# Softmax sums of a cross-attention block inverted on VectorE in four columns instead of as a power on POOL, and P's high part taken one step later on ScalarE

## The chip, the cores and the metric

One core of a Trainium2 chip runs the whole program. The metric is the device time of one execution in microseconds (us). The engines of the core work side by side, each through its own list of instructions in order: TensorE (PE in the profile; PEld is its weight load), VectorE (DVE), ScalarE (ACT), GpSimd (POOL), and SyncE (SP), whose queue issues every DMA of this kernel. They wait for each other only by semaphores.

## The reference

```python
x = x + xattn(layernorm(x), ctx, ctx, w_q, w_k, w_v, w_out, mask)
x = x + ffn(layernorm(x), w12, b12, w3, b3)

def xattn(q, k, v, ...):      # 16 batches, 128 rows, D = 1024, 32 heads of 32, 8 groups of 4 heads
    query, key, value = q @ w_q.T, k @ w_k.T, v @ w_v.T
    scores = einsum('bghnd,bgsd->bghns', query, key) / 32 ** 0.5
    attention = softmax(where(mask, scores, min), axis=-1)
    out = einsum('bghns,bgsd->bghnd', attention, value)
    return out @ w_out.T

def ffn(x, w12, b12, w3, b3): # M = 1024
    x1, x2 = split(x @ w12.T + b12, 2)
    return (silu(x1) * x2) @ w3.T + b3
```

All tensors are float32 with x of (16, 128, 1024). The kernel keeps float32 accuracy by splitting each operand of a product into a high and a low float16 part, and takes three products (high by high, high by low, low by high).

## The kernel before

**Blocks and steps.** The attention part runs over eight blocks of two batches (256 rows). A block has eight steps, one for each group of four heads; g counts the steps of all blocks, 0 to 63. The loop on every engine is the same, for t in 1 to 8 and s in 0 to 7 with g = 8 (t - 1) + s. In round t the attention of block t - 1 is done together with the projections (q, k, v) of block t and the output projection of block t - 2. Behind round 8 comes the feed-forward part.

**One step on TensorE** (L1623 to L1650): the eight score products of g (L1468), a first unit, the product of P and v of step g - 3 (weigh, L1474), and a second unit. A unit is a projection of 24 products. Steps 3 to 6 have one of the output projection, which is twice as long. Step 7 has the two v units and four groups of transposes of new x rows (turn_x, L1415) between them. The results go to five PSUM banks in turn; begin (L1381) waits until the bank's last reader is done. The scores have one PSUM tile only, so the scores of g wait for VectorE to have read those of g - 1 (s_neg, L1465).

**A step's softmax** goes over four engines. The tile e has two buffers, g % 2.
- VectorE masks and scales the scores into e, four heads of a batch u and then four of the other (mask_scores, L1884, instructions L1895). It waits first until the low part of P of g - 2 has been taken from the same buffer (s_plo2, L1893).
- ScalarE takes the exponents (exps, L1201; L1207 where it also sums them into p_sum) for u = 0, then does other work of the step, then u = 1.
- For g in 8 to 47 (NORMED, L72) P is divided by its sum here, scaled by 2**14. In steps 0 and 1 VectorE does it (norm_prob, L1908), in steps 2 to 7 POOL (norm_prob, L975). POOL takes three instructions for each u: p_sum times 2**-14 (L979), that to the power -1 (L981), and the product with e (L985).
- ScalarE takes P's high part (prob_hi, L1213, L1222) at the end of its step g.
- POOL takes the low part (prob_lo, L969, L972) at the head of its step g + 1.
- SP then issues the DMA that transposes both (turn_prob, L727), and TensorE uses them in step g + 3.

**What else stands in the queues.** POOL splits the next block's ctx in steps 0 and 1 (split_ctx, L928, its instructions L904, L906, L908) and takes the rows' roots in steps 2 and 3. SP's list of a step (L786 to L834) puts turn_prob(g - 1) ahead of the step's loads: the q and k stacks, ctx of the next block in step 3, and in rounds 3 to 6 the loads of a piece of the feed-forward weights (load_look) in steps 0, 3 and 5. VectorE takes the maximum of these pieces (max_of, L1729, its instruction L1731) in steps 2, 4 and 6, in its place in the list, ahead of the second unit's low part and of the next mask_scores. ScalarE normalises the next rows with scale_rows (L1295), after prob_hi in steps 4 and 6; the rows are turned by TensorE in step 7.

Of the kernel before, what the change touches and what calls it, by code (L numbers as in the profile page):

```python
# [22 lines left out]
F32 = mybir.dt.float32  # L23
# [8 lines left out]
P = 128  # L32
# [7 lines left out]
U = 2  # L40
# [281 lines left out]

def divided_count(g):

    return g + 1 - normed_count(g)
# [16 lines left out]
def xattn_ffn(nc, x, ctx_t, mask, wq_t, wk_t, wv_t, wo_t, w12_t, b12_t, w3_t, b3_row, out):  # L342
# [8 lines left out]
    with ExitStack() as stack:  # L351
# [82 lines left out]
        inv_pool = part(arena_attn, 60, 1, F32)[:, 0:U * HPG].rearrange("p (u j) -> p u j", u=U)  # L434
        minus_one = part(arena_attn, 62, 1, F32)[:, 0:1]
        inv_vector = part(arena_attn, 61, 1, F32)[:, 0:U * HPG].rearrange("p (u j) -> p u j", u=U)
# [154 lines left out]
        s_minus_one = sem("minus_one_done")  # L591
        s_pinv, s_pnorm = sem("pool_inv_sum_done"), sem("prob_normed_by_pool")
        s_vinv, s_vnorm = sem("vector_inv_sum_done"), sem("prob_normed_by_vector")
# [301 lines left out]
        def _(pool):  # L895
# [57 lines left out]
            pool.memset(minus_one, -1.0).then_inc(s_minus_one, 1)  # L953
            pool.wait_ge(s_minus_one, 1)
# [20 lines left out]
            def norm_prob(g):  # L975
                n = normed_count(g - 1, by_pool)
                for u in range(U):
                    pool.wait_ge(s_exp, 2 * g + u + 1)
                    pool.tensor_scalar(inv_pool[:, u], p_sum[:, g % 2, u], 1 / P_SCALE, None, ALU.mult).then_inc(s_pinv, 1)  # L979
                    pool.wait_ge(s_pinv, 2 * (U * n + u) + 1)  # L980
                    pool.tensor_tensor(inv_pool[:, u], inv_pool[:, u], minus_one.broadcast_to([P, HPG]), ALU.pow)\  # L981
                        .then_inc(s_pinv, 1)
                    pool.wait_ge(s_pinv, 2 * (U * n + u) + 2)
                    heads = e[:, g % 2, u].rearrange("p (j n) -> p j n", j=HPG)
                    ins = pool.tensor_tensor(heads, heads, inv_pool[:, u].rearrange("p (j o) -> p j o", o=1)  # L985
                                             .broadcast_to([P, HPG, SEQ]), ALU.mult)
                ins.then_inc(s_pnorm, 1)

            halves = range(2), range(2, 4)
            for t in range(1, NB + 1):  # L990
                for s in range(STEPS):
                    if GROUPS * (t - 1) + s > PLO_ALONE:
                        prob_lo(GROUPS * (t - 1) + s - 1)
                    if by_pool(GROUPS * (t - 1) + s):
                        norm_prob(GROUPS * (t - 1) + s)
# [84 lines left out]
        def _(act):  # L1080
# [132 lines left out]
            def prob_hi(g):  # L1213
                if by_pool(g):
                    act.wait_ge(s_pnorm, normed_count(g, by_pool))
# [93 lines left out]
            for t in range(1, NB + 1):  # L1309
                for s in range(STEPS):  # L1310
                    g, (tile, tile2) = GROUPS * (t - 1) + s, x_tiles(t, s)
                    exps(g, 0)
                    if t == NB and s - 1 in H_AT:
                        hid_hi(0, H_AT[s - 1])
# [17 lines left out]
                    prob_hi(g)  # L1332
# [345 lines left out]
        def _(dve):  # L1678
# [228 lines left out]

            def norm_prob(g):  # L1908
                n = normed_count(g - 1, by_vector)
                for u in range(U):  # L1910
                    dve.wait_ge(s_exp, 2 * g + u + 1)
                    dve.reciprocal(inv_vector[:, u], p_sum[:, g % 2, u]).then_inc(s_vinv, 1)
                    dve.wait_ge(s_vinv, U * n + u + 1)
                    heads = e[:, g % 2, u].rearrange("p (j n) -> p j n", j=HPG)
                    ins = dve.scalar_tensor_tensor(out=heads, in0=heads, scalar=P_SCALE,
                                                   in1=inv_vector[:, u].rearrange("p (j o) -> p j o", o=1)
                                                   .broadcast_to([P, HPG, SEQ]), op0=ALU.mult, op1=ALU.mult)
# [156 lines left out]
            for t in range(1, NB + 1):  # L2074
# [7 lines left out]
                for s in range(STEPS):  # L2082
                    g, name, (tile, tile2) = GROUPS * a + s, top_at(t, s), x_tiles(t, s)
# [163 lines left out]
```

## Time and profile before

| what | us |
|---|---|
| median of 3 runs | 1074.25 (1072.92 to 1075.79) |
| the profiled execution | 1076.37 |
| its span | 1074.6 |
| PE busy | 1026.1 (95%) |
| VectorE busy | 670.4 (62%) |
| ScalarE busy | 473.2 (44%) |
| POOL busy | 644.7 (60%) |

The span runs from the first to the last instruction; the rest of the profiled time lies around it. Busy is the time in which an engine has an instruction in work. Matmuls are pipelined, so a busy PE is not PE at its peak. The shares are averages over parts with different limits: the feed-forward part fills the second half of the span, and the rounds that the change touches lie between about 113 us and 472 us.

### The profile page before, as it was taken

Reading aid. Unit: us, or ns where it says so; the run is one execution under the profiler, and the core shown is the slowest. Engines: PE = TensorE matmul, PEld = TensorE weight load, DVE = VectorE, ACT = ScalarE, POOL = GpSimd, SP = SyncE. Lnnn points to the kernel's source line nnn. Section 1 sums busy time; section 2 is a strip of 40 time slices with the busy share of each in tenths; the row PEclk is TensorE's granted clock in tenths of the full one; section 3 lists DMA queues with packets and bytes.
Section 4 is the critical chain, followed back from the end, with each engine's and each line's share of the span. In section 5 each row is a group of like instructions: output and inputs, shape, how many; then the busy total and the mean of one; then the engine's idle time right before and its main releaser. Section 6 shows DMA issues by size and latency. Waiting matters only on the chain.

```text
span 1074.6 us, 22142 instructions
## 1 busy us (share of the span) xinstructions
PE 1026.1 (95%) x8320; PEld 683.5 (64%) x8320; DVE 670.4 (62%) x2040; ACT 473.2 (44%) x1303; POOL 644.7 (60%) x657
## 2 busy tenths in 40 slices
PE   8898899998979989989999999999999999999998
PEld 7786757766658557677755544444444788468853
DVE  6889976767677667777856523735766255635431
ACT  5767566656566556666566511123432011301110
POOL 2769877987978879878985879226862201203000
PEclk8998999998999989989999999999999999999999
DMA  9569676897798788969994552397649731774201
GB/s 370 212 171 190 152 193 166 175 249 198 193 219 217 206 210 176 254 173 237 231 255 79 136 218 94 134 271 255 225 164 226 267 113 55 196 238 135 80 30 49
DMA packets 230779, 199.13 MB, mean 185 GB/s; under 512 B 177040, under 2 KB 187280, under 8 KB 225808
## 3 DMA queue, kind: packets, MB, share of 16 engines
q1 hardware_dynamic: 230672, 197.72, 67.1%
q8 instruction: 66, 1.08, 0.4%
q14 instruction: 41, 0.34, 0.1%
HBM read 119.04 MB, written 35.65 MB: 144 GB/s over the span
## 4 chain that ended last, share of the span: by engine, by line
PE 61%; POOL 19%; ACT 5%; DVE 4%; issue 4%; DMA 1%; SPq 1%; DVEq 0%; POOLq 0%; ACTq 0%
PE bank_dense L1411 38%; PE bank_spare L1411 7%; PE bank_score L1567 6%; PE bank_spare L1567 5%; POOL arena_attn L972 5%; POOL arena_attn L981 4%; POOL arena_attn L985 4%; PE bank_av L1567 3%; POOL arena_in L908 2%; ACT arena_attn L1207 2%; POOL arena_in L904 2%; ACT arena_attn L1222 2%; DVE arena_attn L1895 1%; POOL arena_in L906 1%; PE bank_score L1468 1%
## 5 line engine op out<-in xcount | busy, mean ns | idle before, releaser
L1411 PE MATMUL bank_dense<-arena_rows,arena_in 128*128 128x256 f16 (+1 forms) x1272 | 176.1, 296 | 1.6 <-POOL arena_in L908 0.9
L1411 PE MATMUL bank_dense<-arena_attn,arena_rows 128*128 128x512 f16 x768 | 166.4, 379 | 0.0
L1411 PEld LDWEIGHTS bank_dense<-arena_rows,arena_in 128*128 128x128 f16 x1272 | 122.1, 98 | 44.5 <-DVE arena_in L1743 1.3
L1895 DVE CUSTOM_DVE_ANT_0 arena_attn<-bank_score,arena_in 128x128 f32<-128x128 f32 x512 | 143.5, 344 | 0.7 <-PE bank_score L1468 0.5
L1411 PEld LDWEIGHTS bank_dense<-arena_attn,arena_rows 128*128 128x128 f16 x768 | 75.2, 98 | 90.1
L972 POOL TENSOR_TENSOR arena_attn<-arena_attn 128x512 f16<-128x512 f32 x89 | 103.3, 1177 | 46.8 <-ACT arena_attn L1222 46.8
L1207 ACT ACTIVATE arena_attn<-arena_attn,arena_in 128x128 f32<-128x128 f32 x320 | 123.7, 390 | 16.5 <-DVE arena_in L1895 16.5
L1411 PE MATMUL bank_dense<-arena_out,arena_attn 128*128 128x512 f16 x576 | 127.8, 379 | 0.5 <-DVE arena_attn L1937 0.5
L1222 ACT ACTIVATE arena_attn<-arena_attn 128x1024 f16<-128x1024 f32 x64 | 67.5, 1055 | 108.5 <-POOL arena_attn L985 96.8
L1411 PEld LDWEIGHTS bank_dense<-arena_out,arena_attn 128*128 128x128 f16 x576 | 55.5, 98 | 64.0 <-DVE arena_attn L1937 0.6
L1411 PE MATMUL bank_spare<-arena_rows,arena_in 128*128 128x256 f16 (+1 forms) x648 | 87.7, 292 | 0.0
L1411 PE MATMUL bank_dense<-arena_out,arena_in 128*128 128x512 f16 x384 | 83.0, 379 | 0.0
L908 POOL TENSOR_TENSOR arena_in<-arena_in 128x512 f16<-128x512 f32 x62 | 77.1, 1243 | 5.0
L1210 ACT ACTIVATE arena_attn<-arena_attn,arena_in 128x128 f32<-128x128 f32 x192 | 60.8, 391 | 34.1 <-DVE arena_in L1895 33.8
L1411 PEld LDWEIGHTS bank_spare<-arena_rows,arena_in 128*128 128x128 f16 x648 | 62.3, 98 | 19.8
L2000 DVE SCALAR_TENSOR_TENSOR arena_out<-bank_dense,small,arena_out 128x256 f32<-128x256 f32 x64 | 27.9, 478 | 74.9 <-PE bank_dense L1411 74.9
L1411 PEld LDWEIGHTS bank_dense<-arena_out,arena_in 128*128 128x128 f16 x384 | 37.6, 98 | 45.3
L1411 PE MATMUL bank_dense<-arena_in 128*128 128x256 f16 x456 | 64.4, 308 | 1.5 <-DVE arena_in L1750 1.4
L985 POOL TENSOR_TENSOR arena_attn<-arena_attn 128x512 f32<-128x512 f32 x60 | 62.4, 1039 | 4.7
L981 POOL TENSOR_TENSOR arena_attn<-arena_attn 128x4 f32<-128x4 f32 x60 | 62.1, 1035 | 5.0
L918 POOL TENSOR_TENSOR small<-small 128x1 f32<-128x1 f32 x32 | 20.2, 633 | 72.9 <-DVE small L1784 72.9
L1207 ACT ACTIVATION_READ_ACCUMULATOR arena_attn<-arena_attn,arena_in 128x1 f32 x320 | 60.6, 189 | 0.0
(237 smaller groups left out, 1942.1 us busy)
## 6 DMA issues: line engine op xcount, KB each, us to landing
arena_rows<-x SPq DMA_DIRECT2D x32, 512.0 KB, 5.4
arena_in<-w_scratch SPq DMA_DIRECT2D x64, 256.0 KB, 3.0
arena_attn<-q_scratch SPq DMA_DIRECT2D x48, 256.0 KB, 4.3
arena_rows<-w_t SPq DMA_DIRECT2D x12, 1024.0 KB, 6.4
arena_rows<-ctx_t SPq DMA_DIRECT2D x8, 1024.0 KB, 5.9
q_scratch<-arena_attn SPq DMA_DIRECT2D x16, 512.0 KB, 4.6
x_scratch<-arena_rows SPq DMA_DIRECT2D x16, 512.0 KB, 4.1
arena_out<-x_scratch SPq DMA_DIRECT2D x16, 512.0 KB, 5.7
```

What stands on the lines that cost most here:

```text
L904: pool.tensor_tensor(buf, src, spread, ALU.mult).then_inc(s_pool, 1)
L908: pool.tensor_tensor(lo, buf, hi, ALU.subtract).then_inc(ready, 1)
L972: ins = pool.tensor_tensor(p_split[:, g % 2, u, 1], e[:, g % 2, u], p_split[:, g % 2, u, 0], ALU.subtract)
L981: pool.tensor_tensor(inv_pool[:, u], inv_pool[:, u], minus_one.broadcast_to([P, HPG]), ALU.pow)\
L985: ins = pool.tensor_tensor(heads, heads, inv_pool[:, u].rearrange("p (j o) -> p j o", o=1) .broadcast_to([P, HPG, SEQ]), ALU.mult)
L1207: ins = act.activation(head, head, ACT.Exp, bias=neg_max[:, g % 2, h:h + 1], scale=-1.0, accum_out=p_sum[:, g % 2, u, j:j + 1])
L1210: ins = act.activation(head, head, ACT.Exp, bias=neg_max[:, g % 2, h:h + 1], scale=-1.0)
L1222: act.activation(p_split[:, g % 2, :, 0], e[:, g % 2], ACT.Copy).then_inc(s_phi, 1)
L1411: ins = pe.matmul(dst, lhs(a, c), rhs(b, c), start=(c == chunks[0] and n == 0), stop=(c == chunks[-1] and n == 2))
L1567: ins = pe.matmul(seven(v, j), weights[:, a, P * c:P * c + P], rows[:, b, c], start=(c == 0 and n == 0), stop=(c == 3 and n == 2))
L1895: ins = dve.tensor_tensor_reduce(out=e[:, g % 2, h // HPG, SEQ * (h % HPG):SEQ * (h % HPG) + SEQ], in0=B_SCORE[:, SEQ * h:SEQ * h + SEQ], ...
L2000: ins = dve.scalar_tensor_tensor(out=cols, in0=bank("y", f, q)[:, 256 * k:256 * k + 256], scalar=c_ffn[:, 2 * h + k:2 * h + k + 1], in1=co ...
```

## The change

The power on POOL goes, with its constant and its semaphore. VectorE gets a function inv_sums(g, u) with two instructions of four columns: p_sum times 2**-14, and the reciprocal of that. For POOL's steps it is called for u = 0 behind attn_lo in step g, and for u = 1 at the head of step g + 1, ahead of mask_scores. POOL's norm_prob now handles one u per call, with one instruction: u = 0 in step g behind prob_lo(g - 1), u = 1 at the head of step g + 1, ahead of prob_lo(g). On ScalarE prob_hi(g) of POOL's steps moves from the end of step g to step g + 1, behind exps(g + 1, 0). In VectorE's own steps the reciprocal gets the same two instructions, and the product changes from a scalar_tensor_tensor to a tensor_tensor. sums and inv have a buffer for each parity of g.

```diff
@@ POOL
-            def norm_prob(g):
-                n = normed_count(g - 1, by_pool)
-                for u in range(U):
-                    pool.wait_ge(s_exp, 2 * g + u + 1)
-                    pool.tensor_scalar(inv_pool[:, u], p_sum[:, g % 2, u], 1 / P_SCALE, None, ALU.mult).then_inc(s_pinv, 1)
-                    pool.wait_ge(s_pinv, 2 * (U * n + u) + 1)
-                    pool.tensor_tensor(inv_pool[:, u], inv_pool[:, u], minus_one.broadcast_to([P, HPG]), ALU.pow)\
-                        .then_inc(s_pinv, 1)
-                    pool.wait_ge(s_pinv, 2 * (U * n + u) + 2)
-                    heads = e[:, g % 2, u].rearrange("p (j n) -> p j n", j=HPG)
-                    ins = pool.tensor_tensor(heads, heads, inv_pool[:, u].rearrange("p (j o) -> p j o", o=1)
-                                             .broadcast_to([P, HPG, SEQ]), ALU.mult)
-                ins.then_inc(s_pnorm, 1)
+            def norm_prob(g, u):
+                pool.wait_ge(s_vinv, inv_count(g, u))
+                heads = e[:, g % 2, u].rearrange("p (j n) -> p j n", j=HPG)
+                pool.tensor_tensor(heads, heads, inv[:, g % 2, u].rearrange("p (j o) -> p j o", o=1)
+                                   .broadcast_to([P, HPG, SEQ]), ALU.mult).then_inc(s_pnorm, 1)
...
-                    if GROUPS * (t - 1) + s > PLO_ALONE:
-                        prob_lo(GROUPS * (t - 1) + s - 1)
-                    if by_pool(GROUPS * (t - 1) + s):
-                        norm_prob(GROUPS * (t - 1) + s)
+                    g = GROUPS * (t - 1) + s
+                    if by_pool(g - 1):
+                        norm_prob(g - 1, 1)
+                    if g > PLO_ALONE:
+                        prob_lo(g - 1)
+                    if by_pool(g):
+                        norm_prob(g, 0)
@@ ScalarE
             def prob_hi(g):
                 if by_pool(g):
-                    act.wait_ge(s_pnorm, normed_count(g, by_pool))
+                    act.wait_ge(s_pnorm, U * normed_count(g, by_pool))
...
                     exps(g, 0)
+                    if by_pool(g - 1):
+                        prob_hi(g - 1)
...
                     unit_hi(second_unit(t, s))
-                    prob_hi(g)
+                    if not by_pool(g):
+                        prob_hi(g)
@@ VectorE
+            def inv_sums(g, u):
+                dve.wait_ge(s_exp, 2 * g + u + 1)
+                dve.tensor_scalar(sums[:, g % 2, u], p_sum[:, g % 2, u], 1 / P_SCALE, None, ALU.mult).then_inc(s_vsum, 1)
+                dve.wait_ge(s_vsum, inv_count(g, u))
+                dve.reciprocal(inv[:, g % 2, u], sums[:, g % 2, u]).then_inc(s_vinv, 1)
+
             def norm_prob(g):
-                n = normed_count(g - 1, by_vector)
                 for u in range(U):
-                    dve.wait_ge(s_exp, 2 * g + u + 1)
-                    dve.reciprocal(inv_vector[:, u], p_sum[:, g % 2, u]).then_inc(s_vinv, 1)
-                    dve.wait_ge(s_vinv, U * n + u + 1)
+                    inv_sums(g, u)
+                    dve.wait_ge(s_vinv, inv_count(g, u))
                     heads = e[:, g % 2, u].rearrange("p (j n) -> p j n", j=HPG)
-                    ins = dve.scalar_tensor_tensor(out=heads, in0=heads, scalar=P_SCALE,
-                                                   in1=inv_vector[:, u].rearrange("p (j o) -> p j o", o=1)
-                                                   .broadcast_to([P, HPG, SEQ]), op0=ALU.mult, op1=ALU.mult)
+                    ins = dve.tensor_tensor(heads, heads, inv[:, g % 2, u].rearrange("p (j o) -> p j o", o=1)
+                                            .broadcast_to([P, HPG, SEQ]), ALU.mult)
...
+                    if by_pool(g - 1):
+                        inv_sums(g - 1, 1)
                     if g >= 3:
                         divide(g - 3)
                     mask_scores(g)
...
                     if by_vector(g):
                         norm_prob(g)
+                    elif by_pool(g):
+                        inv_sums(g, 0)
```

## Rows read from the trace of the kernel before

**Rows 1.** Windows: round 5, and its late v product (busy by engine, clock, DMA).

```profile
319.85:391.43 71.58, 65.64 (x659) 46.75 (x659) 49.76 (x191) 43.16 (x164) 59.88 (x69) 0.95 0.82 209
...
394.75:399.70 4.95, 4.95 (x26) 3.33 (x24) 1.99 (x4) 2.30 (x10) 3.16 (x4) 0.54 1.04 285
```

**Rows 2.** Groups by line on POOL: busy us, mean ns, idle before.

```profile
L981 POOL TENSOR_TENSOR arena_attn<-arena_attn 128x4 f32<-128x4 f32 x60 | 62.1, 1035 | 5.0
```

**Rows 3.** Waits in round 5: us, times, longest.

```profile
ACT arena_attn L1222 <- POOL arena_attn L985: 21.3, 5, 6.6
```

**Rows 4.** Timeline of PE in rounds 2 and 5: start, us, instruction.

```profile
173.03 0.61 PE L1468 MATMUL bank_score<-arena_attn 96*128 96x128 f16 x8
...
185.33 0.62 PE L1468 MATMUL bank_score<-arena_attn 96*128 96x128 f16 x8
...
328.37 0.62 PE L1468 MATMUL bank_score<-arena_attn 96*128 96x128 f16 x8
...
383.25 0.61 PE L1468 MATMUL bank_score<-arena_attn 96*128 96x128 f16 x8
...
383.81 2.78 PE L1411 MATMUL bank_spare<-arena_in 128*128 128x256 f16 x24
...
391.57 0.66 PE L1420 MATMUL bank_spare<-arena_in,arena_rows 128*128 128x128 f32 x4 [3.22 <-ACT arena_rows L1298]
393.84 1.11 PE L1420 MATMUL bank_spare<-arena_in,arena_rows 128*128 128x128 f32 x4 [1.61 <-DVE v_low L1865]
394.75 5.01 PE L1411 MATMUL bank_dense<-arena_in 128*128 128x256 f16 x24
...
400.00 0.62 PE L1468 MATMUL bank_score<-arena_attn 96*128 96x128 f16 x8
```

**Rows 5.** Timeline of POOL: the low parts of P at four steps.

```profile
329.57 2.28 POOL L972 TENSOR_TENSOR arena_attn<-arena_attn 128x512 f16<-128x512 f32 x2 [2.51 <-ACT arena_attn L1222]
...
347.54 2.27 POOL L972 TENSOR_TENSOR arena_attn<-arena_attn 128x512 f16<-128x512 f32 x2
...
356.04 2.27 POOL L972 TENSOR_TENSOR arena_attn<-arena_attn 128x512 f16<-128x512 f32 x2 [0.39 <-ACT arena_attn L1222]
...
373.10 2.27 POOL L972 TENSOR_TENSOR arena_attn<-arena_attn 128x512 f16<-128x512 f32 x2 [1.17 <-ACT arena_attn L1222]
```

**Rows 6.** Timeline of ACT in round 5.

```profile
330.72 0.40 ACT L1207 ACTIVATE arena_attn<-arena_attn,arena_in 128x128 f32<-128x128 f32 x1 [1.23 <-DVE arena_in L1895]
...
332.28 0.36 ACT L1184 ACTIVATE arena_attn<-bank_dense 128x256 f16<-128x256 f32 x1
...
354.91 1.06 ACT L1222 ACTIVATE arena_attn<-arena_attn 128x1024 f16<-128x1024 f32 x1 [6.64 <-POOL arena_attn L985]
...
391.43 0.39 ACT L1207 ACTIVATE arena_attn<-arena_attn,arena_in 128x128 f32<-128x128 f32 x1
```

**Rows 7.** Timeline of DVE: small operations, masks and maxima of round 5.

```profile
329.51 0.35 DVE L1895 CUSTOM_DVE_ANT_0 arena_attn<-bank_score,arena_in 128x128 f32<-128x128 f32 x1
...
333.54 0.69 DVE L1915 SCALAR_TENSOR_TENSOR arena_attn<-arena_attn 128x512 f32<-128x512 f32 x1
...
334.48 0.18 DVE L1912 RECIPROCAL arena_attn<-arena_attn 128x4 f32<-128x4 f32 x1 [0.24 <-ACT arena_attn L1207]
334.69 1.11 DVE L1915 SCALAR_TENSOR_TENSOR arena_attn<-arena_attn 128x512 f32<-128x512 f32 x1
...
351.11 0.34 DVE L1895 CUSTOM_DVE_ANT_0 arena_attn<-bank_score,arena_in 128x128 f32<-128x128 f32 x1
...
369.59 2.29 DVE L1731 TENSOR_REDUCE arena_in<-arena_rows 128x1 f32<-128x2048 f32 x1 [2.85 <-DMA arena_rows<-w_t]
...
385.07 2.29 DVE L1731 TENSOR_REDUCE arena_in<-arena_rows 128x1 f32<-128x2048 f32 x1 [0.95 <-DMA arena_rows<-w_t]
...
387.61 0.34 DVE L1895 CUSTOM_DVE_ANT_0 arena_attn<-bank_score,arena_in 128x128 f32<-128x128 f32 x1
...
401.14 0.35 DVE L1895 CUSTOM_DVE_ANT_0 arena_attn<-bank_score,arena_in 128x128 f32<-128x128 f32 x1
```

More of the change, by code:

```diff
@@ L320, in normed_count, with inv_count @@
     return sum(kind(n) for n in range(g + 1))
+def inv_count(g, u):
+    return U * normed_count(g - 1) + u + 1
 def divided_count(g):
@@ L433, in xattn_ffn @@
         p_sum = part(arena_attn, 59, 1, F32)[:, 0:2 * U * HPG].rearrange("p (r u j) -> p r u j", r=2, u=U)
-        inv_pool = part(arena_attn, 60, 1, F32)[:, 0:U * HPG].rearrange("p (u j) -> p u j", u=U)
-        minus_one = part(arena_attn, 62, 1, F32)[:, 0:1]
-        inv_vector = part(arena_attn, 61, 1, F32)[:, 0:U * HPG].rearrange("p (u j) -> p u j", u=U)
+        sums = part(arena_attn, 60, 1, F32)[:, 0:2 * U * HPG].rearrange("p (r u j) -> p r u j", r=2, u=U)
+        inv = part(arena_attn, 61, 1, F32)[:, 0:2 * U * HPG].rearrange("p (r u j) -> p r u j", r=2, u=U)
         k_stack = part(arena_attn, 63, 4).rearrange("p (b g n) -> p b g n", b=2, g=4)
@@ L590, in xattn_ffn @@
         s_av, s_inv, s_avread = sem("av_done"), sem("inv_sum_done"), sem("attn_ready")
-        s_minus_one = sem("minus_one_done")
-        s_pinv, s_pnorm = sem("pool_inv_sum_done"), sem("prob_normed_by_pool")
-        s_vinv, s_vnorm = sem("vector_inv_sum_done"), sem("prob_normed_by_vector")
+        s_pnorm, s_vnorm = sem("prob_normed_by_pool"), sem("prob_normed_by_vector")
+        s_vsum, s_vinv = sem("sum_scaled"), sem("inv_sum_of_prob_done")
         s_scales, s_cout = sem("block_scales_done"), sem("c_out_done")
@@ L952, in _ @@
             pool.memset(minus_half[:, :], -0.5).then_inc(s_ones, 1)
-            pool.memset(minus_one, -1.0).then_inc(s_minus_one, 1)
-            pool.wait_ge(s_minus_one, 1)
             pool.memset(ones[:, :], 1.0).then_inc(s_ones, 1)
```

## The prediction

> **What bounds the kernel now.** I read the windows first, then POOL's groups, the waits, and last the timelines of one round, from head to end. I take round 5 for all four rounds 3 to 6, which have the same list of work. In round 5 the first mask_scores starts at 329.51 us and that of the next round at 401.14 us [rows 7], 71.63 us apart. No engine is full: POOL has 59.88 us of work in the round, and TensorE 65.64 us [rows 1]. ScalarE waits 21.3 us in five pieces to take P's high part, each time for POOL's product [rows 3]. So the round is set by a chain that goes over POOL and back over ScalarE. TensorE pays for it in one place. From step 0 to step 7 it needs 54.88 us; step 7 takes 16.75 us, of which it idles 3.22 us for scale_rows, which stands behind prob_hi on ScalarE, and 1.61 us for v's low part [rows 4]. The v product behind these gaps takes 5.01 us where the one ahead of them took 2.78 us [rows 4], and the granted clock in it is 0.54, which is the 1.2 GHz level [rows 1]. Without the gaps and at full clock, step 7 would be 16.75 - 4.83 - 2.23 = 9.7 us, and TensorE alone would make the round 64.6 us. That is the most that can be won, 7.0 us a round.
>
> **What is removed.** The power, 60 times 1.035 us [rows 2], 12 of them a round, is 12.4 us a round of POOL's work, all on its present chain. The multiplication ahead of each goes too. If nothing took their place, the round would come close to TensorE's 64.6 us.
>
> **What is added.** VectorE gets two small instructions for each of 12 batch halves a round. The nearest row is its reciprocal of the same four columns: it starts at 334.48 us and the next instruction at 334.69 us [rows 7]. I take 0.2 us for each of the two, 0.4 us a call; bounds 0.15 us if they overlap and 0.25 us if POOL disturbs them. The product in VectorE's own steps becomes a tensor_tensor. The present one takes 0.69 or 1.11 us [rows 7]; I take no difference, since tile and operands stay the same size, and up to 0.4 us a product either way, four a round.
>
> **What is moved, and its wait.** This decides. prob_hi(g) now stands behind exps(g + 1, 0), and these wait for mask_scores(g + 1). So P's low part of g can't be ready before the next step's mask has started plus this chain: 1.21 us to the first exponent, 1.56 us for four of them [rows 6, 7], 1.06 us for prob_hi and 0.07 us to POOL [rows 5, 6], 2.27 us for prob_lo [rows 5]. That is 6.17 us. Before, prob_hi(g) was often done by then: the low part of step 7 ended 2.34 us after the first mask of the next round [rows 5, 7]. Behind POOL's prob_lo stands SP's turn_prob, and behind that, in SP's list, the loads of ctx and of the weight pieces. Behind these loads wait VectorE's maxima (L1731), and behind a maximum the next mask. It is a closed loop. Counted from the first mask of a round (0), it goes so:
> - Low part of step 7 ready: 6.17 (before 2.34).
> - Both halves of split_ctx and two low parts on POOL. Before, from 331.85 to 349.81 us [rows 5], 17.96 us. None of it changes: 24.1.
> - The mask of step 3 waits for the last of them, to 24.2. VectorE's own way there was 21.60 us before [rows 7] and gets 1.06 us for a prob_hi ahead of exps(g, 1), four small multiplications of 0.2 us and two calls of 0.4 us, 24.3 in all. The two ways end together; I take 24.3.
> - Low part of step 2: 6.17 more, 30.5 (before 358.31 us, 28.80).
> - Transpose, ctx load, weight load, landed. Before, from 358.31 to 369.59 us, 11.28 us [rows 5, 7]: 41.8.
> - Maximum and the second unit's low part, then mask of step 5. From a maximum to its next mask 2.54 us [rows 7], and 0.4 us for the new call: 44.7. That is 2.1 us later than now, 40.08 + 2.54.
> - Low part of step 4, 6.17 more: 50.9 (before 375.37 us, 45.86).
> - Transpose and the second weight load, before from 375.37 to 385.07 us, 9.70 us [rows 5, 7]: 60.6.
> - Maximum, new call, mask of step 7, 2.94 us: 63.5 (before 58.10).
> - From there to the next round's first mask it took 13.53 us [rows 7]. In it ScalarE's exponents started at 391.43 us instead of 1.21 us after the mask, which is 2.61 us of waiting for POOL and scale_rows [rows 6, 7]. These go. prob_hi now stands between the exponents and v's high part, 1.06 us, and a call of inv_sums ahead of the mask, 0.4 us: 12.4, so 75.9.
>
> The round gets 75.9 - 71.6 = 4.3 us longer. POOL saves 12.4 us of work, but the loop passes POOL only where the saving isn't: the split, and the low parts. The moved scale_rows frees TensorE's 3.22 us gap, but in its place TensorE waits for bank and mask: step 6 needs the mask of step 5 to end, 2.1 us later than now, and step 7 the banks that VectorE frees behind the maximum.
>
> Whether v's second product runs at half clock again is open. TensorE still idles ahead of it, for VectorE's read of the turned maximum and for v's low part, so I take 5.01 us. At 2.78 us the round is 73.7. The Trainium skill (TensorE: Matmul & The Clock Gate, Part 1) says that the array's clock passes at half rate unless the engine's recent activity releases it. By that rule, idling ahead of the product keeps it at half rate and the round is 75.9; without the rule it would be 73.7. The trace agrees with the rule here, with 0.54 behind the two gaps [rows 1, 4].
>
> Four rounds, 3 to 6, give +17.2 us. Round 2 has no weight pieces, so no such loop. Its step 7 takes 12.30 us [rows 4] against 9.7 without gaps, of which I take 2.6 us as won, and its VectorE, which sets the first three steps, gets 0.8 + 0.4 us. That is -1.4 us. The sum is +15.8 us. Against the profiled execution's 1076.37 us this is 1092; against the median of the runs, 1074.25, it is 1090.
>
> **The rivals.**
> - *Loop closed, but full clock.* 4 x 2.1 - 1.4 = +7.0 us, 1081. For it: rows show the drop only behind two gaps close together. Against: more gaps than before.
> - *A sum that comes out even.* The parts with transfers are 21.0 us of the loop, and both come from one round. If the first takes 9.70 us like the second (-1.6 us) and the clock stays full (-2.2 us), the round is 72.1, and the time 1074.25 + 4 x 0.5 - 1.4 = 1075: no change.
> - *Faster: the loads leave the loop.* The place is VectorE's wait for the weight piece in steps 4 and 6, 2.85 and 0.95 us now [rows 7]. If both pieces land before VectorE comes to them, the masks of steps 5 and 7 are no longer late, and only TensorE's 64.6 us and some bank waits are left. With 67 to 69 us a round, that is 4 x 3.6 + 1.4 = 16 us less, 1058. It decides this way once the two transfers together take over 4 us less of their 21.0. For it: the DMA engines' share in the round is 0.82 [rows 1], so the loads have some room to run faster. Against: the low parts of steps 2 and 4 come 1.7 and 5.0 us later than now, and today VectorE waits for both pieces already.
> - *Not doing what it says* is hardly possible: the power is off POOL whatever else happens.
>
> **How the numbers follow.** Loop with half clock 0.48, loop with full clock 0.15, even 0.10, faster 0.27. A measurement can tell about 0.3% here, 3.2 us, so the first two count as slower, 0.63, the third as same, 0.10. Forecast 1090. Its own range is 1084 to 1096: 0.15 to 0.25 us for 8 small instructions on the loop is 1.6 us over four rounds, the products of VectorE 0.4 us each on VectorE's way to the mask of step 3, up to 1.6 us a round. The full range goes down to 1062, so that it holds part of the faster case.
>
> **What would show it.** Right: L1731 waits longer for its DMA in steps 4 and 6 (about 4 and 3 us in place of 2.85 and 0.95), prob_hi no longer waits for POOL, POOL's busy time falls by at least the power's 62.1 us, rounds are 75 to 76 us apart, and the scores of step 6 wait for L1895. Wrong: rounds of 65 to 69 us, a granted clock of 1.00 at the end of each round, or L1731 without waits.

## The result and the profile after

The changed kernel takes 1106.2 us (median of 4 runs, 1104.9 to 1106.9), the one before 1074.65 us beside it: ratio 1.0294, 95% interval 1.0276 to 1.0311. It is slower, as forecast, but by 31.6 us where the sum said 15.8, and it lies outside the range of 1062 to 1096 us.

The page after, its busy time by engine:

```profile
span 1104.1 us, 22161 instructions
...
PE 1036.3 (94%) x8320; PEld 683.6 (62%) x8320; DVE 708.6 (64%) x2180; ACT 473.2 (43%) x1303; POOL 568.2 (51%) x536
```

The windows of round 5, from its first mask to that of round 6, and of v's second product [rows 1]:

```profile
342.36:420.74 78.38, 67.59 (x661) 46.95 (x660) 58.74 (x219) 43.02 (x162) 44.40 (x44) 0.93 0.75 191
414.50:419.10 4.60, 4.60 (x27) 3.17 (x24) 2.09 (x6) 2.20 (x10) 1.53 (x2) 0.60 0.70 154
```

POOL's work in the round went from 59.88 to 44.40 us, and VectorE's rose by 9.0 us, from 49.76. Sixteen multiplications and twelve more reciprocals at 0.16 and 0.18 us would be 4.7. The waits of the round:

```profile
ACT arena_attn L1204 <- DVE arena_in L1895: 26.7, 8, 7.4
POOL arena_attn L973 <- ACT arena_attn L1219: 16.0, 6, 2.7
POOL arena_attn L980 <- DVE arena_attn L1912: 14.9, 5, 6.2
DVE arena_in L1731 <- DMA arena_rows<-w_t: 7.0, 2, 5.1
ACT arena_attn L1219 <- DVE arena_attn L1919: 6.2, 2, 3.5
...
PE bank_score L1468 <- DVE arena_in L1895: 4.0, 3, 2.5
...
PE bank_spare L1420 <- DVE small L1693: 2.2, 1, 2.2
```

prob_hi (L1219 now) no longer waits for POOL [rows 3]; POOL waits for it, and ScalarE and TensorE wait for VectorE's masks (L1895). The groups of the new line and of POOL's product:

```profile
L980 POOL TENSOR_TENSOR arena_attn<-arena_attn 128x512 f32<-128x512 f32 x60 | 63.3, 1055 | 79.9 <-DVE arena_attn L1912 79.9
L1910 DVE TENSOR_SCALAR arena_attn<-arena_attn 128x4 f32<-128x4 f32 x80 | 36.9, 462 | 0.2
```

The four-column multiplication takes 462 ns in the mean, not 0.2 us, and its own line says how far that mean is from any one of them (min/median/max):

```profile
L1910 DVE TENSOR_SCALAR arena_attn<-arena_attn x80: 157/226/1123, 119.1 to 498.3; 128x4 f32<-128x4 f32 x80
```

VectorE's timeline over the first steps of round 5, and POOL's over the same stretch:

```profile
347.13 0.28 DVE L1910 TENSOR_SCALAR arena_attn<-arena_attn 128x4 f32<-128x4 f32 x1
347.45 0.18 DVE L1912 RECIPROCAL arena_attn<-arena_attn 128x4 f32<-128x4 f32 x1
347.67 1.39 DVE L1919 TENSOR_TENSOR arena_attn<-arena_attn 128x512 f32<-128x512 f32 x1
348.98 1.00 DVE L1910 TENSOR_SCALAR arena_attn<-arena_attn 128x4 f32<-128x4 f32 x1
350.01 0.18 DVE L1912 RECIPROCAL arena_attn<-arena_attn 128x4 f32<-128x4 f32 x1
...
355.25 1.12 DVE L1910 TENSOR_SCALAR arena_attn<-arena_attn 128x4 f32<-128x4 f32 x1
...
357.93 1.00 DVE L1910 TENSOR_SCALAR arena_attn<-arena_attn 128x4 f32<-128x4 f32 x1
...
364.19 1.11 DVE L1910 TENSOR_SCALAR arena_attn<-arena_attn 128x4 f32<-128x4 f32 x1
```

```profile
346.24 2.27 POOL L973 TENSOR_TENSOR arena_attn<-arena_attn 128x512 f16<-128x512 f32 x2 [2.73 <-ACT arena_attn L1219]
348.47 1.48 POOL L907 TENSOR_TENSOR arena_in<-arena_rows,small 128x512 f32<-128x512 f32 x1
350.02 0.61 POOL L909 CAST arena_in<-arena_in 128x512 f16<-128x512 f32 x1
...
357.41 1.49 POOL L907 TENSOR_TENSOR arena_in<-arena_rows,small 128x512 f32<-128x512 f32 x1
```

The multiplication that starts at 348.98 us ends at 349.98; POOL's L907 ends at 349.95. The one of 357.93 ends at 358.93; POOL's L907 at 358.90. They end with POOL's instruction, whatever their own 0.16 us. So it is in the whole trace: 40 of the 80 took 0.28 to 1.12 us, and each of these ended 0.02 to 0.03 us behind an instruction of POOL; the 24 that met none took at most 0.17 us. The other 16 took 0.16 us beside a running one: six met its last 0.08 us, and ten met L921 on POOL, which has one column. The reciprocal right behind takes 0.18 us each time. The Trainium skill (SBUF — State Buffer, Who interferes with whom) says that VectorE in a two-port mode and GpSimd exclude each other for a whole instruction, the later one blocked entirely. The trace agrees with a wait for a whole instruction, with 1.00 and 1.12 us for work of 0.16; which mode the multiplication ran in no trace shows, and beside L921 it did not wait.

POOL's low parts of steps 2 and 4, the masks of steps 3, 5 and 7 and the next round's first with the two maxima between them, and TensorE's step 7 [rows 4, 5, 7]:

```profile
373.85 2.27 POOL L973 TENSOR_TENSOR arena_attn<-arena_attn 128x512 f16<-128x512 f32 x2 [2.58 <-ACT arena_attn L1219]
...
394.60 2.27 POOL L973 TENSOR_TENSOR arena_attn<-arena_attn 128x512 f16<-128x512 f32 x2 [2.73 <-ACT arena_attn L1219]
```

```profile
369.96 0.35 DVE L1895 CUSTOM_DVE_ANT_0 arena_attn<-bank_score,arena_in 128x128 f32<-128x128 f32 x1
...
387.85 2.29 DVE L1731 TENSOR_REDUCE arena_in<-arena_rows 128x1 f32<-128x2048 f32 x1 [5.08 <-DMA arena_rows<-w_t]
...
390.72 0.35 DVE L1895 CUSTOM_DVE_ANT_0 arena_attn<-bank_score,arena_in 128x128 f32<-128x128 f32 x1
...
405.96 2.29 DVE L1731 TENSOR_REDUCE arena_in<-arena_rows 128x1 f32<-128x2048 f32 x1 [1.93 <-DMA arena_rows<-w_t]
...
408.84 0.35 DVE L1895 CUSTOM_DVE_ANT_0 arena_attn<-bank_score,arena_in 128x128 f32<-128x128 f32 x1
...
420.74 0.35 DVE L1895 CUSTOM_DVE_ANT_0 arena_attn<-bank_score,arena_in 128x128 f32<-128x128 f32 x1
```

```profile
411.44 1.09 PE L1420 MATMUL bank_spare<-arena_in,arena_rows 128*128 128x128 f32 x4 [2.19 <-DVE small L1693]
413.42 1.11 PE L1420 MATMUL bank_spare<-arena_in,arena_rows 128*128 128x128 f32 x4 [0.90 <-DVE v_low L1865]
414.33 4.67 PE L1411 MATMUL bank_dense<-arena_in 128*128 128x256 f16 x24
```

From first scores to first scores, rounds 3 to 6 took 78.87, 77.93, 78.39 and 77.95 us (before 71.47 to 71.63), together 26.8 us more. Round 2 took 0.8 less and what lies ahead of it 0.5 less, round 7 took 71.51 in place of 67.60 us, and from round 8 on both kernels need the same 535.4 us. That is the 29.5 us between the two profiled spans.

### The profile page after: what moved, and what is told of

Its sections match the earlier page's. It is cut to its first block, busy times and chain, and to the rows that moved or that the text cites. A ratio compares the mean times of both kernels' runs of the same rounds, so it can differ in the third digit from the quotient of the medians.

```text
span 1104.1 us, 22161 instructions
## 1 busy us (share of the span) xinstructions
PE 1036.3 (94%) x8320; PEld 683.6 (62%) x8320; DVE 708.6 (64%) x2180; ACT 473.2 (43%) x1303; POOL 568.2 (51%) x536
## 4 chain that ended last, share of the span: by engine, by line
PE 61%; DVE 16%; DMA 7%; ACT 6%; issue 3%; SPq 2%; POOL 2%; DVEq 0%; ACTq 0%; POOLq 0%
PE bank_dense L1411 38%; PE bank_spare L1411 7%; PE bank_score L1567 5%; PE bank_spare L1567 5%; DMA arena_rows<-w_t 5%; DVE arena_attn L1895 4%; ACT arena_attn L1204 3%; PE bank_av L1567 3%; DVE arena_in L1731 2%; DVE arena_attn L1910 2%; POOL arena_attn L973 2%; ACT arena_attn L1219 1%; DVE arena_attn L1919 1%; DVE arena_attn L1865 1%; SPq L736 1%
## 5 line engine op out<-in xcount | busy, mean ns | idle before, releaser
L1411 PE MATMUL bank_dense<-arena_rows,arena_in 128*128 128x256 f16 (+1 forms) x1272 | 180.4, 300 | 1.7 <-POOL arena_in L911 1.0
L1895 DVE CUSTOM_DVE_ANT_0 arena_attn<-bank_score,arena_in 128x128 f32<-128x128 f32 x512 | 143.8, 346 | 0.4 <-PE bank_score L1468 0.4
L1411 PE MATMUL bank_dense<-arena_out,arena_attn 128*128 128x512 f16 x576 | 137.7, 400 | 4.6 <-DVE arena_attn L1937 4.6
L1411 PEld LDWEIGHTS bank_dense<-arena_out,arena_attn 128*128 128x128 f16 x576 | 57.8, 102 | 76.4 <-issue 13.3
L1219 ACT ACTIVATE arena_attn<-arena_attn 128x1024 f16<-128x1024 f32 x64 | 67.1, 1048 | 29.2 <-DVE arena_attn L1919 28.8
L1411 PE MATMUL bank_dense<-arena_in 128*128 128x256 f16 x456 | 60.1, 295 | 1.5 <-DVE arena_in L1750 1.4
L921 POOL TENSOR_TENSOR small<-small 128x1 f32<-128x1 f32 x32 | 19.9, 622 | 81.0 <-DVE small L1784 80.9
L1731 DVE TENSOR_REDUCE arena_in<-arena_rows 128x1 f32<-128x2048 f32 x19 | 43.1, 2270 | 26.1 <-DMA arena_rows<-w_t 26.1
```

What stands on the lines that cost most here:

```text
L1219: act.activation(p_split[:, g % 2, :, 0], e[:, g % 2], ACT.Copy).then_inc(s_phi, 1)
L1411: ins = pe.matmul(dst, lhs(a, c), rhs(b, c), start=(c == chunks[0] and n == 0), stop=(c == chunks[-1] and n == 2))
L1731: dve.tensor_reduce(w_max[:, col(name, i)], src, AX_X, ALU.max, apply_absolute_value=True).then_inc(s_max, 1)
L1895: ins = dve.tensor_tensor_reduce(out=e[:, g % 2, h // HPG, SEQ * (h % HPG):SEQ * (h % HPG) + SEQ], in0=B_SCORE[:, SEQ * h:SEQ * h + SEQ], ...
```

## The experiments

The theory is that the chain of the prediction holds, and that a multiplication on VectorE costs the rest of POOL's running instruction on top. Its rivals: VectorE's number of instructions costs, whatever they are; the move alone costs it all; or the loads have no part in it. Each expectation gives its own letters to them. The table gives for each kernel the time, the ratio to the kernel before on the same chip with its interval, and for round 5 the start of the mask of step 3 and of the next round's first mask, both counted from the round's first mask, as L1895's rows (another line number in some kernels) give them. "Own" is the high part and POOL's second product in their own step, "ahead" the two weight loads ahead of the turn of P in SP's queue.

| | multiplication | high part | loads | us | ratio | mask 3 | round 5 |
|---|---|---|---|---|---|---|---|
| before | POOL, with the power | own | behind | 1074.6 | 1 | 21.60 | 71.63 |
| changed | VectorE | moved | behind | 1106.2 | 1.029 | 27.60 | 78.38 |
| 1 | none | moved | behind | 1087.2 | 1.0111 [1.0093, 1.0129] | 24.44 | 74.72 |
| 2 | VectorE | own | behind | 1093.9 | 1.0175 [1.0158, 1.0192] | 27.21 | 75.87 |
| 3 | POOL, power | moved | behind | 1096.4 | 1.0185 [1.0165, 1.0205] | 24.42 | 76.28 |
| 4 | VectorE | moved | ahead | 1079.3 | 1.0035 [1.0022, 1.0047] | 27.61 | 71.85 |
| 5 | none | own | behind | 1076.0 | 1.0016 [1.0000, 1.0032] | 22.50 | 71.34 |
| 6 | VectorE, twice | moved | behind | 1105.8 | 1.0293 [1.0268, 1.0317] | 27.60 | 78.52 |
| 7 | VectorE, reciprocal twice | moved | behind | 1108.0 | 1.0305 [1.0277, 1.0332] | 27.59 | 78.73 |
| 8 | VectorE, two tensors | moved | behind | 1106.3 | 1.0292 [1.0265, 1.0319] | 27.58 | 78.08 |
| 9 | none | moved | ahead | 1056.4 | 0.9858 [0.9821, 0.9896] | 24.42 | 67.34 |
| 10 | as before | own | ahead | 1074.3 | 0.9998 [0.9985, 1.0011] | 21.61 | 71.64 |
| 11 | VectorE | moved | ahead, rows too | 1079.4 | 1.0048 [1.0030, 1.0065] | 27.58 | 71.30 |
| 12 | none | own | ahead, rows too | 1052.1 | 0.9793 [0.9779, 0.9807] | 22.49 | 64.91 |
| 13 | ScalarE | moved | behind | 1093.8 | 1.0184 [1.0164, 1.0205] | 25.01 | 75.09 |
| 14 | ScalarE | moved | ahead | 1063.9 | 0.9898 [0.9881, 0.9914] | 25.02 | 68.21 |
| 15 | VectorE | own | ahead | 1080.4 | 1.0048 [1.0029, 1.0067] | 27.22 | 72.03 |
| 16 | ScalarE | own | ahead, rows too | 1058.8 | 0.9854 [0.9839, 0.9869] | 22.89 | 67.19 |

**1. Without the multiplication.** P_SCALE is 1, so P isn't scaled, and the reciprocal is taken of the sums themselves.

```
-P_SCALE = 2.0 ** 14
+P_SCALE = 1.0
-                dve.tensor_scalar(sums[:, g % 2, u], p_sum[:, g % 2, u], 1 / P_SCALE, None, ALU.mult).then_inc(s_vsum, 1)
-                dve.wait_ge(s_vsum, inv_count(g, u))
-                dve.reciprocal(inv[:, g % 2, u], sums[:, g % 2, u]).then_inc(s_vinv, 1)
+                dve.reciprocal(inv[:, g % 2, u], p_sum[:, g % 2, u]).then_inc(s_vinv, 1)
```

> The changed kernel with P_SCALE = 1, so that VectorE's multiplication of four columns goes in every step and only the reciprocal is left; P is not scaled by 2**14. Theory A (two costs: the multiplication waits for POOL's running instruction, some 1 us each in steps 0 to 2, and P's high part is late by a mask and four exponents, which a closed loop through the weight loads repeats): the mask of step 3 comes about 3.4 us earlier after the round's first mask, at 24.2 instead of 27.6 us, where POOL's chain takes over; rounds of about 74 us instead of 78.3, in all about 1088 us. Theory B (the moved high part alone makes the loss, the multiplication is hidden): 1103 us or more. Theory C (the port wait alone makes the loss): about 1072 us.

A: 1087.2. The mask of step 3 falls by 3.2 us, to 24.44, and the round by 3.7.

**2. The high part and POOL's second product back in their own step.** The calls prob_hi(g - 1) and norm_prob(g - 1, 1) go, and prob_hi(g) and norm_prob(g, 1) stand in step g as before.

> The changed kernel with prob_hi back at the end of its own step on ScalarE, and POOL's second product back in its own step; reciprocals stay on VectorE with their multiplication. Theory A: P's low part is ready about 4 us after the next mask's start instead of 6.17, in each of the three places of the loop, so rounds of about 73 us and 1082 us in all. Theory B: 1070 us or less, since nothing else cost anything. Theory C: no change, about 1104 us.

1093.9 is what none of them said. The mask of step 3 hardly moves, 27.21 us, since the multiplications stay. P's low part of step 2 is ready 4.59 us behind that mask, not about 4, where it was 6.16 in the changed kernel. The round is 2.5 us shorter, 2.1 of them behind the mask of step 3.

**3. The move alone,** the power still on POOL.

> The kernel before with the move alone: prob_hi behind the next step's first exponents, POOL's product split over two steps, but the power still on POOL and nothing new on VectorE. Theory A and theory B: the loop closes here too and POOL's powers are added to it, rounds of about 77 us, 1099 to 1102 us in all. Theory C: no loss, 1070 to 1078 us.

A little under the forecast, 1096.4; that a move alone is harmless is refuted. The mask of step 3 is at 24.42, 3.2 us ahead of the changed kernel's: with no multiplication on VectorE the two ways end where the prediction had them end.

**4. The loads ahead of the turn,** in SP's list:

```
+                    if 3 <= t < 7 and s == 3:
+                        load_look(look_at(t, 4), w3_t[t - 3])
+                    if 3 <= t < 7 and s == 5:
+                        load_look(look_at(t, 6), w12_t[2 * (t - 3) + 1])
                     if g >= 1:
                         turn_prob(g - 1)
```

> The changed kernel with SP's weight piece loads of steps 3 and 5 ahead of that step's turn of P instead of behind it. Theory A: VectorE's waits for the pieces (26.1 us in eight) nearly vanish, the loop is no longer closed through the transfers, rounds of 71 to 73 us, 1076 to 1086 us in all. If the loop does not run over these loads: 1102 to 1108 us.

A: 1079.3, 27 us back. The mask of step 3 is as late as before (27.61), but the round is 71.85 us, and L1731 has no wait for a DMA in it. The closed loop over the loads is shown.

**5. Edits 1 and 2 together.**

> The changed kernel with P not scaled (the multiplication of the sums is left out, VectorE takes the reciprocal alone), and with POOL's second product and the high part back in their own step. The kernel without the multiplication alone took 1087.2, the one with the high part back alone 1093.9. A, the small multiplications beside POOL delay the mask of step 3 by 3.3 us a round and the moved high part delays the low parts by some 2 to 4 us a round, and the two add: low parts come sooner than in the kernel before, since POOL no longer takes the power (its 2.2 us a step), the mask of step 3 stands about 22 us after the round's first mask, rounds 69.5 to 71.5 us apart, 1066 to 1076. B, VectorE's work, whichever way it is placed, sets the round: 1083 or more, rounds over 74 us apart. C, the two edits overlap (the smaller hides behind the larger): 1083 to 1087.

A, at its upper edge: 1076.0. With both costs gone and no power on POOL the kernel is just where it was before.

**6 to 8. What is it about the small instruction?** A second multiplication, a second reciprocal, each into columns nobody reads; and the multiplication as a tensor_tensor with a constant column.

```
                 dve.tensor_scalar(sums[:, g % 2, u], p_sum[:, g % 2, u], 1 / P_SCALE, None, ALU.mult).then_inc(s_vsum, 1)
+                dve.tensor_scalar(spare[:, g % 2, u], p_sum[:, g % 2, u], 1 / P_SCALE, None, ALU.mult)
```

> The changed kernel with a second four-column multiplication on VectorE behind each of the first, into columns that nobody reads. A, each such instruction waits for POOL's running instruction to end: the second one meets the next instruction of POOL and takes up to 1.0 to 1.1 us more in steps 0 to 3, so the mask of step 3 is later by 2 to 4.5 us and each round by as much, four or five times over: 1114 to 1128. B, it is only one instruction more, at the 0.16 us that the cheapest of them takes: 4 to 6 of them ahead of the mask of step 3, under 1 us a round, 1107 to 1111. C, VectorE's time doesn't bound: 1104 to 1107.

> The changed kernel with a second four-column reciprocal on VectorE for each call, into columns that nobody reads; its twin has a second multiplication in that place. A, a reciprocal doesn't wait for POOL: 0.18 us each, under 1 us a round, 1107 to 1111, while the twin with the multiplication takes 1114 to 1128. B, any small instruction of VectorE beside POOL costs the same: this one and its twin within 2 us of each other.

> The changed kernel with the sums multiplied by a constant column through an instruction with two tensor operands instead of one with a scalar, four columns as before. A, what waits for POOL is the form with one tensor and a scalar: the new form takes about 0.2 us each also beside POOL, mask of step 3 some 3 us sooner, 1086 to 1092 (without any multiplication it was 1087.2). B, every elementwise multiplication of float32 in SBUF waits for POOL, only the reciprocal doesn't: again up to 1.0 to 1.1 us each, 1103 to 1110.

The lines of the two multiplications of 6, of the second reciprocal of 7, and of the two-tensor form of 8 (min/median/max in ns):

```profile
L1911 DVE TENSOR_SCALAR arena_attn<-arena_attn x80: 156/286/1143, 118.7 to 498.3; 128x4 f32<-128x4 f32 x80
L1912 DVE TENSOR_SCALAR arena_attn<-arena_attn x80: 153/158/172, 119.7 to 498.4; 128x4 f32<-128x4 f32 x80
```

```profile
L1912 DVE RECIPROCAL arena_attn<-arena_attn x80: 162/166/173, 120.3 to 499.3; 128x4 f32<-128x4 f32 x80
```

```profile
L1914 DVE TENSOR_TENSOR arena_attn<-arena_attn x80: 149/280/1159, 119.1 to 496.0; 128x4 f32<-128x4 f32 x80
```

My expectation for 6 was wrong: the second multiplication never took over 172 ns, and 6 and 7 are within the measurement of the changed kernel. Kernel 7 lies in its A's 1107 to 1111, 2.2 us above its twin where B had at most 2, and since the twin didn't come to 1114 the two times don't decide between them; the instructions' own times do. So it isn't the number of small instructions. It also isn't "each one waits": the first waits for the end of POOL's instruction, and the second falls into the gap. In 6 the timelines of VectorE and POOL show it:

```profile
350.41 1.00 DVE L1911 TENSOR_SCALAR arena_attn<-arena_attn 128x4 f32<-128x4 f32 x1
351.33 0.16 DVE L1912 TENSOR_SCALAR arena_attn<-arena_attn 128x4 f32<-128x4 f32 x1
```

```profile
349.90 1.48 POOL L908 TENSOR_TENSOR arena_in<-arena_rows,small 128x512 f32<-128x512 f32 x1
351.45 0.61 POOL L910 CAST arena_in<-arena_in 128x512 f16<-128x512 f32 x1
```

L908 ends at 351.38 us, the first multiplication at 351.41, the second has started at 351.33 and POOL's next starts at 351.45. What is paid is one of POOL's instruction ends per place in the chain.

The reciprocals of 7 stand behind a multiplication too, so by themselves they could owe their 0.17 us to the same gap. In kernel 1 there is no multiplication ahead of the reciprocal, 61 of its 80 start while an instruction of POOL runs, and none takes longer:

```profile
L1910 DVE RECIPROCAL arena_attn<-arena_attn x80: 159/168/179, 118.5 to 480.9; 128x4 f32<-128x4 f32 x80
```

Kernel 8 came out as B said: the two-tensor form reaches 1159 ns too, and of the three forms tried only the reciprocal never does. The Trainium skill (SBUF — State Buffer, SBUF: two separate sides) counts an instruction of VectorE with two inputs in SBUF among those that exclude GpSimd's, when that one reads SBUF; the trace of 8 agrees with it, with up to 1159 ns.

**9, 14. No multiplication, or the multiplication on ScalarE, with the loads ahead; 13, on ScalarE alone.** The scaling stays in 13, 14 and 16:

```
                 ins.then_inc(s_exp, 1)
+                if g in NORMED:
+                    act.wait_ge(s_exp, 2 * g + u + 1)
+                    act.activation(sums[:, g % 2, u], p_sum[:, g % 2, u], ACT.Copy, scale=1 / P_SCALE).then_inc(s_vsum, 1)
```

> The changed kernel with P not scaled (no multiplication of the sums on VectorE) and with the two weight loads of steps 3 and 5 ahead of the turn of P in SP's queue. The one edit alone gave 1087.2, the other 1079.3. A, both act on the same loop (late low part, then the load behind it), and with the load off the loop the rounds are held by PE and VectorE at 71.4 to 71.9 us, so the multiplication costs little there: 1071 to 1079. B, the 3.3 us a round of the multiplications are paid whatever the loads do: 1064 to 1068.

> The changed kernel, P scaled as before, with the four-column multiplication of the sums on ScalarE, behind the exponentials of its call, instead of on VectorE; VectorE takes the reciprocal alone. A, it was the instruction's wait for POOL on VectorE that cost: on ScalarE it takes 0.2 to 0.3 us, nearly as without any multiplication (1087.2): 1087 to 1093, mask of step 3 some 24.5 to 25.5 us after the round's first mask. B, one more instruction between the last exponential and the product costs the same wherever it is: 1102 to 1108.

> The changed kernel, P scaled as before, with the multiplication of the sums on ScalarE and the two weight loads of steps 3 and 5 ahead of the turn of P in SP's queue. A, the same as without the multiplication (1056.4) but for some 0.2 us per call on ScalarE: 1056 to 1063, rounds 65.5 to 67.5 us, PE's granted clock over 0.99. B, the gain without the multiplication came from leaving the scaling out: 1072 to 1080.

The same multiplication, 207 ns in the mean on ScalarE, gives 12.4 us back by itself and 15.4 with the loads ahead. So most of it was the place on VectorE beside POOL, not the scaling. Kernel 13 is 0.8 us over A's range and kernel 14 0.9 us, with a clock of 0.987; without any multiplication it is 6.6 and 7.5 us less again, more than the 0.6 us by which the mask of step 3 differs; what makes up the rest was not settled. Kernel 9 went past both expectations: 1056.4. The windows of its round 5, from first mask to first mask, and of a stretch one round long from the middle of round 5 on:

```profile
314.93:382.27 67.34, 64.57 (x658) 45.33 (x656) 49.88 (x202) 43.72 (x162) 44.37 (x44) 0.97 0.84 220
345.19:410.84 65.65, 63.25 (x662) 45.23 (x659) 48.13 (x199) 42.27 (x155) 42.95 (x44) 1.00 0.83 217
```

TensorE's busy time fell from 67.59 to 64.57 us in round 5, at a granted clock of 0.97, and to 63.25 us in the stretch behind it at 1.00, which is 2.4 GHz throughout. In all of that stretch TensorE waited no longer than 1.0 us at once.

**10, 15. The loads ahead in the kernel before, and with the high part back.**

> The kernel before, with the two weight loads of steps 3 and 5 ahead of the turn of P in SP's queue and nothing else. A, in the kernel before the loads behind the low parts of steps 2 and 4 are on the loop that sets its rounds of 71.5 us, as the prediction had it: the rounds shorten by 1 to 4 us, 1058 to 1071. B, its rounds are as much held by PE's own work and its waits in step 7: 1073 to 1077, the same as before.

> The changed kernel, the multiplication still on VectorE, with POOL's second product and the high part back in their own step and the two weight loads ahead of the turn of P. With the loads ahead alone it was 1079.3, with the high part back alone 1093.9. A, once the loads are off the loop the multiplications beside POOL hold the round (the mask of step 3 stays 27 us after the first mask), and PE's slow clock and waits in step 7 stay: 1073 to 1080. B, the high part's place holds the round then: 1054 to 1066.

10 is B: the maxima's waits are down from 3.8 us to 0.4, and the mask of step 5 comes 2.9 us sooner, yet that of step 6 doesn't (49.35 us in place of 49.34), and ScalarE still waits 21.3 us for POOL [rows 3]. That of step 7 is 0.54 us sooner. TensorE's step 7 in it:

```profile
391.50 1.12 PE L1420 MATMUL bank_spare<-arena_in,arena_rows 128*128 128x128 f32 x4 [3.76 <-ACT arena_rows L1298]
393.77 1.11 PE L1420 MATMUL bank_spare<-arena_in,arena_rows 128*128 128x128 f32 x4 [1.15 <-DVE v_low L1865]
394.68 5.02 PE L1411 MATMUL bank_dense<-arena_in 128*128 128x256 f16 x24
```

The first gap of [rows 4] has grown from 3.22 to 3.76 us and takes up those 0.54. So the rounds before were held twice, by POOL with its power and by the loads: 5 takes out the one and 10 the other, and neither gains; both together do (12 and 16). 15 is 0.4 us over A's range, no better than 4: with the loads off the loop the high part's place is worth nothing while the multiplications stay.

**11. Round 7's row loads ahead too.**

> The changed kernel with the two weight loads ahead of the turn of P in SP's queue (alone 1079.3), and in round 7 also the two loads of x rows of step 0 ahead of it. A, the 3.9 us that round 7 lost are VectorE's wait for rows that were loaded behind the turn of a late P: round 7 falls from 70.3 us to 67 to 68.5, 1076 to 1078. B, what VectorE waited for was hidden or something else is late: round 7 stays at 70 to 71 us, 1079 to 1080.

B: round 7 takes 70.4 us, against 70.3 in kernel 4. Kernel 4 waits for such rows twice, 3.01 us each. The wait for those of step 0 is gone, the one for those of step 4 is still there, and VectorE's masks now wait 4.3 us for POOL's low parts, where it was 0.3:

```profile
523.69 1.28 DVE L1775 BATCH_NORM_STATS2 small<-arena_rows 128x6 f32<-128x512 f32 x2 [3.35 <-DMA arena_rows<-x_scratch]
```

**12, 16. All mends,** without the multiplication, and with it on ScalarE.

> The changed kernel with everything that was found to cost taken out: P not scaled (no multiplication of the sums), POOL's second product and the high part in their own step, the two weight loads and round 7's row loads ahead of the turn of P. VectorE takes the reciprocals, POOL no power. A, rounds are held by PE's work (65.6 us busy in a round) and the waits of step 7 (some 5 us): rounds 69 to 71.5 us, 1060 to 1074. B, another loop of the same length holds the rounds at 71.5 us: 1074 to 1077.

> The changed kernel, P scaled as before, with all the mends: multiplication of the sums on ScalarE, POOL's second product and the high part in their own step, the two weight loads and round 7's row loads ahead of the turn of P. Without any multiplication it took 1052.1. A, 1052 to 1059. B, the scaling costs wherever it is done: 1070 or more.

1052.1 (P not scaled), 8 us below the lower end of A, with rounds of 65 to 67 us, and 1058.8 us, in A's range. Kernel 16 computes all that the kernel before does, 1.5% faster. Their step 7, first of 12 and then of 16:

```profile
375.78 0.66 PE L1416 MATMUL bank_spare<-arena_in,arena_rows 128*128 128x128 f32 x4 [1.53 <-DVE v_low L1861]
376.52 2.79 PE L1407 MATMUL bank_dense<-arena_in 128*128 128x256 f16 x24
```

```profile
379.87 0.66 PE L1419 MATMUL bank_spare<-arena_in,arena_rows 128*128 128x128 f32 x4 [1.79 <-DVE v_low L1864]
380.63 4.40 PE L1410 MATMUL bank_dense<-arena_in 128*128 128x256 f16 x24
```

The gap is 0.26 us longer, the product behind it 1.61 us: most of the 2.3 us between the two rounds is TensorE's clock, not ScalarE's work. In round 4 of kernel 16 the same product took 2.79 us, and that round, from first scores to first scores, took 65.93 us, against 65.27 in kernel 12.

## Why the prediction was half right

Its loop, term by term, from the rows of round 5 (T0 = 342.36 us):

| | forecast | measured | step, forecast | step, measured |
|---|---|---|---|---|
| low part of step 7 | 6.17 | 6.15 | 6.17 | 6.15 |
| mask of step 3 | 24.3 | 27.60 | 18.1 | 21.45 |
| low part of step 2 | 30.5 | 33.76 | 6.17 | 6.16 |
| first load landed | 41.8 | 45.49 | 11.28 | 11.73 |
| mask of step 5 | 44.7 | 48.36 | 2.94 | 2.87 |
| low part of step 4 | 50.9 | 54.51 | 6.17 | 6.15 |
| second load landed | 60.6 | 63.60 | 9.70 | 9.09 |
| mask of step 7 | 63.5 | 66.48 | 2.94 | 2.88 |
| next round | 75.9 | 78.38 | 12.4 | 11.90 |

- **The step that failed** is "I take 0.2 us for each of the two", bounds 0.15 to 0.25 us. Six multiplications stand ahead of the mask of step 3, at 0.28, 1.00, 1.12, 1.00, 1.11 and 0.16 us: 4.67 us where I counted 1.2, so 3.5 us, and the mask came 3.3 us late. The four products beside them, where I took no difference, went from 4.44 to 4.68 us. I took the price from the reciprocal, the nearest row by size and engine. It was the wrong neighbour: it never waits. A tensor_scalar of exactly this shape stood in the trace of before, and its line there reads:

```profile
L1941 DVE TENSOR_SCALAR small<-small x8: 229/229/1074, 115.2 to 647.6; 128x4 f32<-128x4 f32 x8
```

  "0.25 us if POOL disturbs them" had no row behind it; this one would have set that bound at 1.07 us.
- **The loop itself held.** Every other step is within about 0.6 us, and kernel 1, which takes the failed term out, has its mask of step 3 at 24.44 us (forecast 24.3), its round at 74.72 us (75.9) and its time at 1087.2 us, inside the range of the likeliest case. Kernel 4 shows that the loop closes over the loads.
- **Half clock** came, 0.60 in the product's window and 4.67 us, and in all four rounds (4.01 to 5.20 us). Idling ahead of the product isn't enough for it by itself, as the last section shows. So the first rival is out, and the even sum too: the two transfers took 20.8 us together, where it needed 19.4.
- **The faster rival** was the mechanism's mirror image: it would have needed transfers of 4 us less. When the loads are taken off by hand and the multiplications too, its 67 to 69 us a round and its 1058 us do come: rounds of 65.7 to 69.0 us and 1056.4, 1063.9 and 1058.8 us in kernels 9, 14 and 16.
- **Round 7** the sum put at nothing, without a reason, and it missed 3.9 us. It has no such weight loads, but SP loads rows of x there behind the same late turn. VectorE waited 3.9 us for them (1.9 before), TensorE twice behind VectorE, and the longest is:

```profile
512.88 1.29 DVE L1775 BATCH_NORM_STATS2 small<-arena_rows 128x6 f32<-128x512 f32 x2 [3.08 <-DMA arena_rows<-x_scratch]
```

  Kernel 11 shows that this one wait isn't the whole of it. In kernels 2, 5 and 15, with the high part in its own step, round 7 took 69.2 to 69.5 us, with it moved 70.2 to 74.1; what else holds it was not settled.
- **Round 2** gained 0.8 us, not 1.4, and 0.5 us came ahead of it. One profile can't tell these apart: kernels 4 and 11, with the same instructions up to there, took 71.66 and 72.76 us for round 2.
- **What would show it:** L1731 waits 5.08 and 1.93 us (forecast about 4 and 3); POOL's busy time fell by 76.5 us, from 644.7; rounds are 78 to 79 us apart, not 75 to 76; the scores of step 6 wait 1.27 us for L1895.

In sum, forecast 15.8 us, measured 29.5 between spans: 9.6 more in rounds 3 to 6 (2.4 each: 3.3 of the multiplications, less 0.5 us in the tail and 0.4 in the other terms), 3.9 in round 7, and 0.1 in the rest. The medians are 2.1 us further apart than the profiled spans.

## What to carry to other kernels

Price a small instruction of VectorE by a row of its own form beside a busy POOL, and look at the longest of that row, not the mean: here 0.16 us became up to 1.12, by what was left of POOL's instruction. Moving a producer later costs what is queued behind its consumers: here two weight loads that stood behind the turn of P, and putting them ahead was worth 27 us in the changed kernel and nothing in the one before. Where two loops of like length hold a round, each mend alone shows nothing; try them together before dropping either.

## What the runs showed that I had not expected

- A multiplication of four columns on VectorE ends with POOL's running instruction (349.98 and 349.95 us), and a second one right behind it costs 0.16 us and adds nothing to the round (27.60 us to the mask of step 3 with one and with two).
- A reciprocal of the same columns never took over 0.18 us beside POOL, the two-tensor form up to 1.16. Nor is it the operation alone: a tensor_scalar on one column never waited either, in the kernel before:

```profile
L1784 DVE TENSOR_SCALAR small<-small x32: 143/149/155, 5.7 to 930.5; 128x1 f32<-128x1 f32 x32
```

  No run tests which property of an instruction makes it wait.
- v's product ran at 2.79 us behind a gap of 1.53 us, and at 4.40 behind one of 1.79 us. The gap's length doesn't decide it: kernel 16 had 2.79 us behind 1.80 us in round 4, kernel 12 had 4.44 us behind 1.53 us in round 2. No run separates what does.
